# Mamba's opening: late sums split after the first decayed blocks, and one more copy of B and C on the DVE

## The reference, cut to what matters

```python
dt = softplus(x @ W_dt.T + b_dt)            # 16 heads
A  = -exp(A_log) * dt
B  = (x @ W_B.T).reshape(b, L, 16, 64)
C  = (x @ W_C.T).reshape(b, L, 16, 64)
X  = x_in.reshape(b, L, 16, 8) * dt[..., None]
# per head: Y[l] = sum over s <= l of (C[l] . B[s]) * exp(sum of A over s+1..l) * X[s]
y  = (Y.reshape(b, L, d) * silu(z)) @ W_out.T
```

## Time and profile before

| | us |
|---|---|
| median of three runs | 722.4 |
| the three runs | 722.32, 722.4, 727.2 |
| the profiled execution | 725.93 |
| its span | 724.0 |

### The profile page before, as it was taken

How to read it: one execution, slowest core, us unless ns; L and a number is a source line. 1 busy time by engine, 2 the same in 40 slices (tenths; PEclk the granted TensorE clock), 3 DMA queues, 4 the chain that set the end, 5 groups by cost and what they waited for, 6 DMA issues and landing times. The chain is left out here.

```text
span 724.0 us, 12388 instructions
## 1 busy us (share of the span) xinstructions
PE 678.0 (94%) x4100; PEld 506.0 (70%) x4100; DVE 571.1 (79%) x1309; ACT 418.5 (58%) x756; POOL 324.7 (45%) x404
## 2 busy tenths in 40 slices
PE   6899998697899999999999797999999998999997
PEld 5677774544467777777778586777777775777785
DVE  5789978899979888987988964666666676889774
ACT  4557676885246555556656674555555555555553
POOL 2658883201237766465668362220413200555463
PEclk9999999999999999999999996999999999999999
DMA  6635430000013232222313000000000000323141
GB/s 170 199 102 176 148 97 1 0 1 1 1 59 118 72 105 103 75 66 82 89 59 101 18 1 1 2 2 2 1 2 0 0 1 2 117 74 117 55 122 43
DMA packets 34329, 43.16 MB, mean 60 GB/s; under 512 B 5216, under 2 KB 17504, under 8 KB 34272
## 3 DMA queue, kind: packets, MB, share of 16 engines
q1 hardware_dynamic: 34272, 42.46, 19.0%
HBM read 41.13 MB, written 1.31 MB: 59 GB/s over the span
## 5 line engine op out<-in xcount | busy, mean ns | idle before, releaser
L697 POOL TENSOR_TENSOR p_prod<-p_p,p_gate_row 128x512 f32<-128x512 f32 x128 | 203.8, 1603 | 108.4 <-DVE p_p L504 64.2
L384 ACT ACTIVATE p_sil<-p_ps_a 128x512 f32<-128x512 f32 x176 | 105.3, 599 | 134.4 <-PE p_ps_a L100 130.8
L509 DVE TENSOR_TENSOR p_hlo<-p_prod,p_hhi 128x512 fp32r<-128x512 f32 x176 | 149.3, 849 | 0.3 <-ACT p_hhi L393 0.2
L504 DVE TENSOR_TENSOR p_p<-p_sil,p_ps_b 128x512 f32<-128x512 f32 x128 | 87.1, 681 | 53.3 <-ACT p_sil L384 38.7
L393 ACT CAST p_hhi<-p_prod 128x512 fp32r<-128x512 f32 x176 | 108.1, 615 | 20.9 <-POOL p_prod L697 20.8
L98 PE MATMUL p_ps_a<-xt_hi,w_uphi 128*128 128x512 f32 x176 | 74.3, 422 | 0.0
L98 PE MATMUL p_ps_acc<-p_hhi,w_downhi 128*128 128x512 f32 x176 | 71.3, 405 | 1.2 <-DVE p_hlo L509 1.0
L98 PE MATMUL p_ps_b<-xt_hi,w_uphi 128*128 128x512 f32 x176 | 70.9, 403 | 0.8 <-DVE p_prod L504 0.7
L100 PE MATMUL p_ps_b<-xt_hi,w_uplo 128*128 128x512 f32 x176 | 70.3, 399 | 0.0
L99 PE MATMUL p_ps_a<-xt_lo,w_uphi 128*128 128x512 f32 x176 | 70.1, 398 | 0.0
L100 PE MATMUL p_ps_a<-xt_hi,w_uplo 128*128 128x512 f32 x176 | 70.0, 398 | 0.0
(11 more groups left out here) (356 smaller groups left out, 1424.4 us busy)
## 6 DMA issues: line engine op xcount, KB each, us to landing
p_gate_row<-gate_rows SPq DMA_DIRECT2D x128, 256.0 KB, 3.3
w_rawbuf<-in_L_ffn_fc_w_dram SPq DMA_DIRECT2D x3, 512.0 KB, 6.3
w_rawbuf<-in_L_ffn_w_dram SPq DMA_DIRECT2D x3, 512.0 KB, 5.4
out_dram<-x SPq DMA_DIRECT2D x4, 256.0 KB, 3.5
w_rawbuf<-in_L_ffn_shared_w_dram SPq DMA_DIRECT2D x3, 256.0 KB, 5.0
x<-in_L_attn_x_dram SPq DMA_DIRECT2D x2, 256.0 KB, 3.6
x<-in_L_attn_x_dram SPq DMA_DIRECT2D x1, 512.0 KB, 8.7
mb_xraw<-in_L_attn_W_B_dram SPq DMA_DIRECT2D x1, 512.0 KB, 4.6
```

The source lines that it names most:

```text
L384: nc.scalar.activation(sil[:, u % 2], ps_a[:, u % 2], ACT.Silu).then_inc(c["sil"].sem, 1)
L504: nc.vector.tensor_tensor(dst, sil[:, u % 2], ps_b[:, u % 2], ALU.mult).then_inc(c["p1"].sem, 1)
L509: nc.vector.tensor_tensor(hlo[:, u % R], prod[:, u % R], hhi[:, u % R].bitcast(F32), ALU.subtract).then_inc(c["hlo"].sem, 1)
L697: G.tensor_tensor(prod[:, u % R], p1[:, u % 2], gate_row[:, e % ROWS], ALU.mult).then_inc(c["prod"].sem, 1)
```

## The change

Four edits, all in the opening and in the first section:

1. ACT no longer takes piece 3 (`take_bc(0, 0, 3)`). The DVE takes it, after `step_sizes`.
2. ACT's `take_ends(0, 1, 2)` therefore comes right after piece 2.
3. The DVE's `split_sums` and `split_decays` of the late tiles leave the opening. They come after the two decayed blocks of group 0 of the first section, and `widen_late` goes from group 0 to group 1.
4. In ACT's first section `widen_high(0)` and `widen_high(1)` go behind the `take_bc` of their group.

```diff
 ACT, section:
-                    if first and q < 2:
-                        widen_high(q)
                     if first and q == 1:
                         take_ends(1, 2, BATCH)
                     if group and q == (3 if first else 0):
...
                     if more:
                         take_bc(1 - h, m + 1, q, half(q, 2))
+                    if first and q < 2:
+                        widen_high(q)
 ACT, opening:
             take_bc(0, 0, 2, ps_c[0])
-            take_bc(0, 0, 3, ps_c[1])
             take_ends(0, 1, 2)
 DVE:
+            def split_late():
+                head.split_sums(dve, 1, BT, TILES)
+                split_decays(1, BT, TILES)
 DVE, section:
                     if first and q == 0:
+                        split_late()
+                    if first and q == 1:
                         widen_late()
 DVE, opening:
             head.step_sizes(dve, 1, BT, TILES)
-            head.split_sums(dve, 1, BT, TILES)
-            split_decays(1, BT, TILES)
+            take_bc(0, 0, 3, ps_c[1])
             section(0, 0, first=True, group=1)
```

## The result

| | median us | runs | ratio to before, 95% interval |
|---|---|---|---|
| before | 722.4 (720.82 to 727.2) | 7 | |
| changed | 718.17 (717.23 to 719.5) | 7 | 0.9935 [0.9909, 0.9961] |

The changed kernel is 0.65% faster; the forecast was 719.2 us, in a range from 714.5 to 722.0. Not only the median moved: the runs of before lie 6.4 us apart, those of the changed kernel 2.3. Its profiled execution has a span of 715.3 us, against 724.0.

The account below looks back on a forecast made before the run. Bound: PE's 3.90 us wait for the DVE's decayed block and the half clock behind it. Half clock 5.7 us plus shorter chain 1.4 gave 718.8 from the profile; weighed against the median, 719.2, range 714.5 to 722.0.

Parts of the forecast that it names:

- Steps 1 and 2: Opening: DVE's copy of piece 3 takes 1.22 us; first cap 2.65 us earlier, PE idle 1.0 us, not 3.9.
- Step 3: Clock behind PE's first gap: the fall at 438.46 is gone, granted clock 1.00 from 433 to 465 us.
- Step 4: DVE's cut behind group 0's decayed blocks: 2.7 us instead of 4.32, up to 0.8 us later if POOL's small instructions hold it.
- Step 5: Group 1: the cut lies bare for 1.0 us; piece 1 starts at 442.35 in place of 448.59.
- Step 6: ACT's `widen_high(1)` makes group 2's exponential 0.7 us late; piece 2 at 447.9 in place of 455.02, -7.1 us.
- Against the median: Profile read as 3.5 us above the 722.4 median; median runs taken to pay 1.7 us of half clock, not 5.7.
- Rival B: Whole kernel: profiling adds a constant 3.5 us and all runs before paid the long stretch; 715.3 us, chance 0.22.
- C: Opening: the runs at 722.4 had no half clock here, only the shorter chain is left; 721.0 us, chance 0.12.
- Rival D: Group 1: cut still held at 4.32 us, PE stands 2.1 us, clock falls one group later; 726.5 us, chance 0.08.

Follow-up runs that it names:

- Fill_before: Kernel before plus fifteen unread matmuls on PE where it waits for the first decayed block: 720.08 us, 0.9931 of before; repeated, 719.83 us, 0.9945.
- copy_only: Kernel before with only piece 3's copy moved from ACT to the DVE, ahead of the cut: 726.83 us, 1.0035 of before.
- delay4: Changed kernel with four extra caps on the DVE ahead of the first one, lengthening PE's gap: 723.81 us, 1.0002 of before.
- split_only: Changed kernel, but ACT takes piece 3 as before, ahead of the exponentials: 719.85 us, 0.9939 of before.
- delay2: Changed kernel with two extra caps on the DVE ahead of the first one: 722.24 us, 0.9988 of before.

## Why the prediction was right

**What bounds the kernel.** Right. The half clock was read as a second cost, apart from the wait, and as the larger one: 5.7 us of the 7.1. Fill_before takes away only this one and measures 5.78, profile against profile.

**The terms of the chain.** Compared at full clock, that is, the changed kernel against fill_before, from one caps line to the next, in us:

| from | filled | changed | difference | predicted |
|---|---|---|---|---|
| DVE's first copy to first caps | 6.96 | 4.26 | -2.70 | -2.65 |
| to the caps of group 1 | 4.87 | 5.65 | +0.78 | +1.0 |
| to the caps of group 2 | 5.21 | 4.85 | -0.36 | -0.45 |
| to the caps of group 3 | 4.94 | 5.35 | +0.41 | +0.7 |
| sum | 21.98 | 20.11 | -1.87 | -1.4 |

Steps 1 and 2 hold within 0.1 us: the copy of 1.23 us, the cap right behind it, a gap of 1.06 us. Step 3 holds: 1.00 from 425 to 465. Step 4 was mis-sized by 0.3 us: the cut takes 2.41 us, not 2.7, because its first two instructions take 0.25 and 0.26 us, and 0.35 had been taken from forms with two inputs. That the two long ones of the earlier trace rows were held by POOL is confirmed from the other side by copy_only: there the first instruction meets POOL's large one and takes 1.00 us, and the second, which had taken 1.09, takes 0.34. (They end beside POOL's large ones, not exactly with them: the second of the earlier trace rows ends at 434.82, POOL's at 434.59.) By the Trainium skill, "SBUF — State Buffer", section "SBUF: two separate sides", one of the two engines shuts the other out for a whole instruction; the trace agrees as far as these large ones go, with 1.00 to 1.09 us beside them and 0.25 to 0.26 without. That POOL's small ones would hold the cut in its new place did not happen. Only four of them still lie beside it, and there it was POOL that took longer: 0.99 us for the four, from 434.63, where they took 0.84. Step 5 has the bare part of the cut right in kind; it is 0.78 us. Step 6 names the right wait, but took it for 0.7 us where it costs 0.42 (2.45 us from the cap to the decayed block, and not 2.03). The exponential of group 2 starts 1.22 us after the cap, where 1.4 had been worked out:

```profile
443.46 0.63 ACT L2066 ACTIVATE mb_sm<-mb_sm 128x512 f32<-128x512 f32 x1
```

The copy, the widening and the exponential were strung end to end in the sum, while in the trace each starts some 0.1 us before the one ahead of it has ended.

**Against the median.** The step that carried most risk. It took the profile's 725.93 for one run of many and the median's runs for ones that had paid a shorter stretch of half clock. The direct evidence is in the runs of before, 88 in the four groups, each with its mean granted clock:

| mean clock of the run | runs | median us |
|---|---|---|
| under 0.9845 | 24 | 725.0 |
| 0.9845 to 0.9885 | 30 | 724.3 |
| 0.9885 to 0.9935 | 30 | 722.0 |
| over 0.9935 | 4 | 720.3 |

Time and clock go together (correlation -0.82), from 720.03 us to 727.93. Rival B, a constant of the profiling, falls with it: the changed kernel's profiled execution is its fastest run, 717.23. So does C: the runs of before do pay. But the picture of two kinds of run, one with a price of 1.7 us and one with 5.7, was too simple: the mean clocks stand at more than two levels (23 of the 88 runs at 0.992, 18 at 0.987, 21 at 0.984 or 0.985, 7 at 0.982, 4 at 0.995). Where the half clock lies in a run without a profile is not shown; that it can be as short as 3.41 us in this place is shown by delay4 alone.

And the median of 88 runs is 723.7, not 722.4; the filled kernel's 719.84 (18 runs) puts the average price of the half clock at 3.8 us (4.32 and 4.05 within the two groups). So the forecast came within 1.0 us of 718.17 partly by luck. Its starting point, the median of three runs, stood 1.3 us below that of the 88, which pulls it down. The 1.7 us of clock that it took off were 2.1 us too few and the 1.4 us of chain 0.5 us too few, which both push it up. With the measured terms the same sum is 723.7 - 3.8 - 1.9 = 718.0, and the changed kernel's median over its 25 runs in three groups is 718.7.

**Rival D** did not happen, but its mechanism is real, and about 2 us fits the runs: 1.74 us of idle PE kept the clock in the profile of split_only, 2.17 lost it in that of delay2. These are one profile each, so the exact point is not shown, nor that it is the same in every run. The changed kernel's 1.06 us kept the clock in three profiles of three.

## What to carry to other kernels

Where a slice of the page shows a low clock, look for the idle time of PE ahead of it and price both: here 2.8 us less of waiting came with 1.9 us less of chain, and the clock was worth on the average about twice that. Work of an engine that has no reader for a while belongs behind the instruction that PE waits for, even where it then lies bare again for most of a microsecond. And when a few runs of a kernel scatter by more than their change, the mean clock of each run tells whether they are the same program at different luck: compare many of them, or compare a stretch of the trace.

## What the runs showed that was not expected

The length of the half clock does not follow the length of the gap: 3.41 us behind 3.36 us of idle PE, 10.24 behind 2.17 and behind 4.26, 13.66 behind 3.90. With PE busy for 13.03 of 13.66 us, or for 10.24 of 10.24 in delay2, the clock did not come back at once. And fifteen matmuls of no use at all, 3.77 us of work, made the kernel of before as fast as the change did, within what the runs can tell (0.9931 and 0.9945 against 0.9935 and 0.9945).
